# A transformer block with top-2 experts: normalisations moved to GpSimd, ranks by two products, and small changes of order

## The reference

```
x = x + attention(layernorm(x))      # 16 heads of 128, rope, causal softmax, output projection
x = x + ffn(layernorm(x))            # router over 8 experts, the best 2 of them, and a shared expert
layernorm(x) = (x - mean) / sqrt(var + 1e-5)
ffn(x):  scores = softmax(x @ gate_w.T); the top 2 scores, divided by their sum, weigh
         (silu(x @ w1[e]) * (x @ w3[e])) @ w2[e], experts 176 wide;
         plus (silu(x @ sw1) * (x @ sw3)) @ sw2, 352 wide
```

## Time and profile before

| what | value |
|---|---|
| median of 3 runs | 728.51 us (728.29 to 728.64) |
| time of the profiled execution | 729.91 us |
| its span, first to last instruction | 727.9 us |
| TensorE busy, products | 716.8 us, 98% |
| TensorE busy, weight loads | 690.7 us, 95% |
| VectorE / ScalarE / GpSimd busy | 617.2 (85%) / 526.8 (72%) / 506.2 us (70%) |
| mean granted clock of TensorE | 0.998 of full speed |

### The profile page before, as it was taken

One profiled execution on the slowest core, in us unless ns is written; L12 is line 12 of the kernel. 1 busy time (PEld: TensorE's weight loads), 2 busy tenths in 40 slices (PEclk: granted clock), 3 DMA queues, 4 the chain that ended last, 5 costly groups with the idle time before them and its releaser, 6 DMA issues.

```text
span 727.9 us, 16486 instructions
## 1 busy us (share of the span) xinstructions
PE 716.8 (98%) x5490; PEld 690.7 (95%) x5490; DVE 617.2 (85%) x1774; ACT 526.8 (72%) x1664; POOL 506.2 (70%) x531
## 2 busy tenths in 40 slices
PE   7999999999999999999999999999999999999997
PEld 6999999999999999999999999999999989999997
DVE  5888899989998999899989898989898976776657
ACT  5787777777777777777777777777777765666564
POOL 5898467787777777877777777777767623544545
PEclk9999999999999999999999999999999999999999
DMA  6555213221422143214321421131454373344383
GB/s 213 155 176 166 86 31 138 108 88 37 136 106 87 45 135 117 79 46 143 116 77 44 143 106 56 43 103 38 140 205 162 138 270 113 118 123 126 109 292 107
DMA packets 51211, 85.91 MB, mean 118 GB/s; under 512 B 8632, under 2 KB 43416, under 8 KB 49528
## 3 DMA queue, kind: packets, MB, share of 16 engines
q1 hardware_dynamic: 47080, 73.44, 30.3%
q0 software_dynamic: 4048, 11.42, 4.4%
HBM read 60.12 MB, written 44.59 MB: 144 GB/s over the span
## 4 chain that ended last, share of the span: by engine, by line
PE 80%; DVE 8%; POOL 6%; ACT 2%; issue 2%; DMA 1%; SPq 1%; POOLq 0%; DVEq 0%
PE bank L662 60%; PE bank L712 5%; PE bank L702 3%; PE bank L721 3%; POOL work L489 3%; DVE work L1104 2%; POOL rows_by_expert L1917 2%; DVE work L1097 1%; POOL qkt_lo L1788 1%; PE bank L954 1%; PE bank L935 1%; PE bank L704 1%; DVE xn L1261 1%; PE bank L849 1%; ACT work L1553 1%
## 5 line engine op out<-in xcount | busy, mean ns | idle before, releaser
L489 POOL TENSOR_TENSOR work<-work 128x512 f32<-128x512 f32 x127 | 164.9, 1298 | 52.7 <-DVE work L1104 51.9
L1788 POOL TENSOR_TENSOR qkt_lo<-work,qkt_hi 128x512 fp32r<-128x512 f32 x112 | 144.8, 1293 | 74.1 <-ACT qkt_hi L1546 74.1
L1104 DVE TENSOR_TENSOR work<-bank,sinn 64x512 f32<-64x512 f32 x256 | 176.2, 688 | 3.4
L662 PE MATMUL bank<-xnt_hi,w_lo 128*128 128x256 f32 x512 | 148.6, 290 | 0.8 <-DVE xnt_lo L1430 0.8
L662 PE MATMUL bank<-xnt_hi,w_hi 128*128 128x256 f32 x512 | 145.2, 284 | 0.0
L662 PE MATMUL bank<-xnt_lo,w_hi 128*128 128x256 f32 x512 | 145.2, 284 | 0.0
L1546 ACT CAST qkt_hi<-work 128x512 fp32r<-128x512 f32 x112 | 69.6, 622 | 87.3 <-POOL work L489 87.1
L1553 ACT ACTIVATE work<-work,bias 128x128 f32<-128x128 f32 (+1 forms) x256 | 112.7, 441 | 0.9 <-DVE bias L1113 0.9
L1097 DVE TENSOR_TENSOR work<-bank,cosn 128x512 f32<-128x512 f32 x128 | 88.0, 687 | 23.5 <-PE bank L662 23.2
L662 PEld LDWEIGHTS bank<-xnt_hi,w_lo 128*128 128x128 f32 x512 | 98.3, 192 | 1.7 <-DVE xnt_lo L1430 1.0
L662 PEld LDWEIGHTS bank<-xnt_hi,w_hi 128*128 128x128 f32 x512 | 98.6, 193 | 0.5
(11 more groups left out here) (205 smaller groups left out, 2125.3 us busy)
## 6 DMA issues: line engine op xcount, KB each, us to landing
rows_by_expert<-in_zero_t SPq DMA_DIRECT2D x17, 1028.0 KB
weights_split<-stage SPq DMA_DIRECT2D x40, 176.0 KB
w_lo<-weights_split SPq DMA_DIRECT2D x4, 1408.0 KB, 9.7
w_lo<-results_by_token SPq DMA_DIRECT2D x16, 256.0 KB, 5.3
w_lo<-rows_by_expert SPq DMA_DIRECT2D x24, 128.5 KB, 2.1
w_hi<-weights_split SPq DMA_DIRECT2D x2, 1536.0 KB, 6.4
stage<-in_L_ffn_w SPq DMA_DIRECT2D x32, 88.0 KB, 2.2
weights_split<-stage SPq DMA_DIRECT2D x20, 128.0 KB
```

The source lines that it names most:

```text
L489: eng.tensor_tensor(roped[:, a], rope_cos[:, a], rope_sin[:, a], ALU.add).then_inc(rope_add, 1)
L662: mm = pe.matmul(out, lhs[a], rhs[b], start=start and n == 0, stop=stop and n == 2, skip_group_check=more)
L1104: op = nc.vector.tensor_tensor(rope_sin[lo:lo + 64, a], p_qk[a][hi:hi + 64, :, :], sn, ALU.mult)
L1788: nc.gpsimd.tensor_tensor(qkt[a][1][:, :, :], roped[:, a], qkt[a][0][:, :, :], ALU.subtract).then_inc(qkt_lo, 1)
```

## The change

- The router's rows of sequence b-1 are normalised by GpSimd, the first half in head 3 and the second in head 4, each between rope sum and low part (in sequence 7 in heads 2 and 3). `rows_norm` on VectorE stays for the last sequence's rows alone.
- The next sequence's rows are normalised by GpSimd in head 10; VectorE keeps sequence 0 (`first_norm`). VectorE waits for the router's norm before it overwrites `mv` in head 5.
- `rsqrt` works in place; the tile `vare` goes.
- `ranks` takes two products instead of four. `member` gets eight more columns, the sum of both halves, by a second GpSimd add in `choose`; the second product reads first half and sum with a stride.
- 14 products on zeros follow the first values, before the scores of head 0.
- Order: in `closing` the low part and the cast of the shared expert's tile 1 come behind those of head 13's probabilities; behind it `low_s(0)`, `mult_s(2)`, `low_s(1)`, `low_x(0)` come before the statistics and aggregates; at the end the second scaled sum of the last tile comes behind `low_s` of that tile.

```diff
-RP = 7
+RP = 8
-WARM = 25
+WARM, AGAIN = 25, 14
-        member = sb("member", [P, ST * E], F32R)
+        member = sb("member", [P, 3 * E], F32R)
+        p_rest = [bank[a][:, E:3 * E] for a in (3, 4, 7)]
             def ranks(n, a):
-                pe.wait_ge(routed, (n - 1) * RP + 4)
+                pe.wait_ge(routed, (n - 1) * RP + 5)
-                first, second = member[:, 0:E], member[:, E:ST * E]
-                pe.matmul(p_rank[a], order[:, 0, :], member[:, :], start=True, stop=False)
-                pe.matmul(p_rank[a][:, E:ST * E], order[:, 1, :], first, start=False, stop=True)
-                pe.matmul(p_total[a], order[:, 1, :], first, start=True, stop=False)
-                pe.matmul(p_total[a], order[:, 1, :], second, start=False, stop=True).then_inc(rank_ps, 1)
+                pe.matmul(p_rank[a], order[:, 0, :], member[:, 0:ST * E], start=True, stop=False, skip_group_check=True)
+                pe.matmul(p_rest[a], order[:, 1, :], member[:, :].rearrange("p (t e) -> p t e", e=E)[:, 0:3:2, :],
+                          start=False, stop=True, skip_group_check=True).then_inc(rank_ps, 1)
+            for _ in range(AGAIN):
+                pe.matmul(bank[7][:, 0:S], pts[0][:, 0, :], pts[0][:, :, :], start=True, stop=True)
...
-                        if h == 2:
-                            rows_norm(b, b - 1)
                         if h == 5:
+                            wait(dve, xn2_done, b)
                             norm_mv(b + 1)
-                        if h == 9:
-                            norm_x(b + 1)
...
+            def row_norm(out, b, t):
+                return nc.gpsimd.tensor_scalar(out, resid[:, b * ST + t, :], mv[:, t, 0:1], rstd[:, t:t + 1],
+                                               ALU.subtract, ALU.mult)
...
+                    if b is not FIRST:
+                        if h + soon == 3 and b is not LAST:
+                            pool.wait_ge(rstd2_done, b)
+                            row_norm(xn2[:, 0, 0:D], b - 1, 0)
+                        if h + soon == 4:
+                            row_norm(xn2[:, 1, 0:D], b - 1, 1).then_inc(xn2_done, 1)
...
+                    if h == 10 and b is not LAST:
+                        pool.wait_ge(rstd_done, b + 2)
+                        row_norm(xn[:, 0, :], b + 1, 0)
+                        row_norm(xn[:, 1, :], b + 1, 1).then_inc(xn_done, 1)
...
+                            if b is LAST:
+                                pool.wait_ge(rstd2_done, b)
+                                row_norm(xn2[:, 0, 0:D], b - 1, 0)
...
+                pool.wait_ge(routed, (n - 1) * RP + 4)
+                nc.gpsimd.tensor_tensor(member[:, ST * E:], member[:, 0:E].bitcast(F32), member[:, E:ST * E].bitcast(F32),
+                                        ALU.add).then_inc(routed, 1)
...
             residual(LAST)
-            rows_stats(B, LAST)
-            rows_mv(B)
             low_s(0)
             mult_s(2)
             low_s(1)
+            low_x(0)
+            rows_stats(B, LAST)
+            rows_mv(B)
             mult_s(3)
-            low_x(0)
...
                 if t >= BY_POOL:
-                    finish(t)
+                    finish_first(t)
+                if BY_POOL <= t < NT - 1:
+                    finish_second(t)
             low_s(NT - 1)
+            finish_second(NT - 1)
```

More of the change, by code:

```diff
@@ L99, in build @@
         mv = sb("mv", [P, ST, 2])
-        vare = sb("vare", [P, ST])
         rstd = sb("rstd", [P, ST])
@@ L1082, in norm_mv, with first_norm @@
                 op.then_inc(mv_done, 1)
[L1084 to L1091, removed]
+            def first_norm():
+                dve.wait_ge(rstd_done, 1)
+                for t, done in enumerate((first_xn, xn_done)):
+                    nc.vector.tensor_scalar(xn[:, t, :], resid[:, t, :], mv[:, t, 0:1], rstd[:, t:t + 1],
+                                            ALU.subtract, ALU.mult).then_inc(done, 1)
             def rope_cosines(h):
@@ L1219, in closing @@
                 attended(12)
-                rows_low(1)
                 plan_tiles(0, 1)
                 probs_then_inverse(13)
+                rows_low(1)
                 biggest(15)
@@ L1294, in reduce_both @@
             def reduce_both(n):
-                dve.wait_ge(routed, (n - 1) * RP + 5)
+                dve.wait_ge(routed, (n - 1) * RP + 6)
                 nc.vector.tensor_reduce(red[:, :, :, :], prod[:, :, :, :].rearrange("p k c (t e) -> p (k c t) e", t=ST),
@@ L1410, in plan_tiles, with finish_first @@
                                                    ALU.add).then_inc(done, 1)
-            def finish(t):
+            def finish_first(t):
                 dve.wait_ge(came[t], 16)
@@ L1416, in finish, with finish_second @@
                                                ALU.mult, ALU.add).then_inc(fin_last, 1)
+            def finish_second(t):
                 dve.wait_ge(fin_last, 2 * (t - BY_POOL) + 1)
@@ L1425, in _ @@
             norm_mv(0)
-            norm_x(0)
+            first_norm()
             split_lo(0)
@@ L1623, in closing @@
                 attended(12)
+                probs_high(13)
                 rows_high(1)
-                probs_high(13)
                 scaled_by(14)
@@ L1781, in rsqrt @@
                 pool.wait_ge(ready_sem, count)
-                nc.gpsimd.tensor_scalar(vare[:, 0:n], mv[:, 0:n, 1], EPS, 1.0, ALU.add, ALU.mult).then_inc(step_sem, 1)
+                nc.gpsimd.tensor_scalar(rstd[:, 0:n], mv[:, 0:n, 1], EPS, 1.0, ALU.add, ALU.mult).then_inc(step_sem, 1)
                 pool.wait_ge(step_sem, count)
-                nc.gpsimd.tensor_tensor(rstd[:, 0:n], vare[:, 0:n], mhalf[:, 0:n], ALU.pow).then_inc(done_sem, 1)
+                nc.gpsimd.tensor_tensor(rstd[:, 0:n], rstd[:, 0:n], mhalf[:, 0:n], ALU.pow).then_inc(done_sem, 1)
+            def row_norm(out, b, t):
+                return nc.gpsimd.tensor_scalar(out, resid[:, b * ST + t, :], mv[:, t, 0:1], rstd[:, t:t + 1],
+                                               ALU.subtract, ALU.mult)
             def low(h):
@@ L1886, in choose @@
                 pool.wait_ge(pick_done, n)
-                nc.gpsimd.tensor_tensor(member[:, :], pick[:, 0, :], pick[:, 1, :], ALU.add).then_inc(routed, 1)
+                nc.gpsimd.tensor_tensor(member[:, 0:ST * E], pick[:, 0, :], pick[:, 1, :], ALU.add).then_inc(routed, 1)
+                pool.wait_ge(routed, (n - 1) * RP + 4)
+                nc.gpsimd.tensor_tensor(member[:, ST * E:], member[:, 0:E].bitcast(F32), member[:, E:ST * E].bitcast(F32),
+                                        ALU.add).then_inc(routed, 1)
             def weigh(n):
```

## The result

The changed kernel takes 731.78 us (median of 5 runs, 731.26 to 732.15), where the kernel before, run beside it, takes 728.51 us: ratio 1.0043, interval [1.003, 1.0055]. It is slower by 3.3 us; forecast was 718.8 us, range 716.9 to 722.3. Its profiled execution took 731.51 us, span 729.7.

What follows compares the result with a forecast made beforehand. TensorE's products were taken to bound the kernel nearly everywhere. 5.2 + 1.8 + 1.3 + 1.3 + 0.4 - 0.3 = 9.7 us off the profiled 729.91 gave 720.2, less 1.40 for the median 718.8; range 716.9 to 722.3.

Steps and rivals of the forecast that it cites:

- the price of the scaling: GpSimd's 128x256 scaling in heads 3, 4 and 10: taken as 0.75 us, between bounds of 0.19 and 0.83.
- the rival with its formula 4d - 3.64: GpSimd scaling far dearer: delay per sequence at price d, gain eaten from 1.26 us, 735.3 at 1.5; chance 0.03.
- signs of being wrong: Waits for GpSimd at heads 3 to 5 and 11 to 14, scaling over 1.2 us, or half rate after 14.5.
- the cover: Slack hiding GpSimd's delay: 0.73 us idle at head 3, 0.69 behind head 4's low part, 1.49 idle at head 10.
- a cover like the 0.69: Head 10: GpSimd 0.5 us later against TensorE was claimed to stay inside slack like that behind head 4's low part.
- Waits of TensorE that go, 5.2 us: TensorE's waits for VectorE's low probabilities: 0.62 in sequence 0, 3.5 at head 3, 1.1 at head 10, all going.
- Ranks, 1.8: Two of four rank products go, eight times 0.22 us, 1.8 us in all, counted in full.
- TensorE is the bound on both sides: Around the rank products TensorE sets the pace before and behind, so their 1.8 us counts in full.
- Idle products, 1.3: At the start 14 products hold the full clock from 14.4 to 18.0, gaining 1.3 us, ends 0 and 1.66.
- The rival: Clock at the start gives nothing, as timed runs kept it or 14 products don't hold it: 720.1 us; chance 0.15.
- Order, 1.3 + 0.4: Reordering gains 1.3 us at the last sequence's passage to the experts (0.35, 0.70, 0.25) and 0.4 at the end.
- Small waits, 0.3: Growing small waits at heads 0 to 2 through GpSimd's sends and sums cost 0.3 us, ends 0 and 1.2.

Runs made afterwards that it cites:

- e6: The kernel before with one dead 128x256 scaling added on GpSimd at head 10 of sequences 1 to 6: 728.18 us, ratio 0.9998.
- e7: The kernel before with two dead 128x256 scalings added on GpSimd at head 10 of sequences 1 to 6: 733.56 us, ratio 1.0068.
- e4: The kernel before with only the 14 products on zeros added: 728.59 us, ratio 1.0002.
- e11: The kernel before with only the ranks by two products and GpSimd's small second add: 727.70 us, ratio 0.9984.
- e12: The kernel before with only the other order, in and behind the last sequence and at the end: 727.11 us, ratio 0.9979.
- e1: The changed kernel with both normalisations back on VectorE at their old heads: 725.64 us, ratio 0.9959.
- e2: The changed kernel with only the next sequence's normalisation back on VectorE, at head 9: 726.91 us, ratio 0.9978.
- e3: The changed kernel with only the router's normalisation back on VectorE, at head 2: 730.72 us, ratio 1.0026.
- e5: The kernel before with ten dead GpSimd operations at its start, five forms at two widths, to time each form: 733.49 us in one execution.
- e8: The changed kernel with both norms on ScalarE, at heads 3 and 10, and a small per-row shift on VectorE: 727.51 us, ratio 0.9983.

## Why the prediction was wrong

The forecast was 13.0 us too low. The move of the norms accounts for 11.0 of it (a cost of 6.1 in place of a gain of 4.9), the idle products for 1.3, the ranks for 0.7.

**The step that failed first is the price of the scaling.** The bounds were 0.19 and 0.83, with 0.75 taken. It is 1.22 us, outside both. The lower row was nearly all start and the upper one an operation of another form; neither bounds a one-input operation with two steps. The bound should have reached past the two-input add, and the rival with its formula 4d - 3.64 should have had far more than 0.03. (A scaling "over 1.2 us" stood among the signs of being wrong, and it came.) At d = 1.22 that formula gives 1.24 us a sequence, 8.7 in all. That takes most of the gain and still ends as slightly faster (718.8 + 8.7 = 727.5), so the price alone does not explain 731.8.

**The second is the cover.** At head 3 I had looked for slack behind the low part of head 4 (0.69) and let head 3's delay run into it. But the scores that read head 3's low part come first. In before that low part ends at 180.69 + 1.29 = 181.98, and this is the load behind the wait for it (the first that reads the low part itself follows 0.22 us later):

```profile
182.44 0.30 PEld L702 LDWEIGHTS bank<-work 128*128 128x128 f32 x2
```

So there is 0.46 of cover, and 0.44 of it existed only because TensorE was itself waiting for `pt_lo` just ahead. Take that wait away and be 0.49 late (1.22 - 0.73): 0.49 + 0.44 - 0.46 = 0.47, the measured loss of head 4. The gain at head 3 was paid back one head later. At head 10 I named what is queued behind GpSimd ("the rope sum, ScalarE's cast, the low part") but allowed it a cover like that of the low part. The path that matters leaves it at the cast: behind the cast ScalarE's queue has the exponentials and `xnt_high`, and the chain above shows each begin as the one ahead of it ends (216.54, 217.16, 217.47, 217.87, 218.74). Then come VectorE's `xnt_lo` and TensorE's first projection of the next sequence, with 0.08 us of cover and not "a cover like the 0.69". Late by 2.44 - 1.49 = 0.95, TensorE earlier by the 0.38 it gained at head 10, less 0.08: 1.25, measured 1.26 over heads 11 and 12. e6 and e7 show it without the change.

**Waits of TensorE that go, 5.2 us: right as far as it went.** They went from 7.2 to 0.3. "All of it goes if nothing else is as late": something was, by up to 1.2 us.

**Ranks, 1.8:** the products went, 0.22 at each place; measured 1.1, since 0.19 came back at head 12 in six sequences (8 x 0.22 - 6 x 0.19 = 0.6 by the trace; the interval of the timing, 0.5 to 1.8, holds both). The second GpSimd add has 8 columns and not 16, and cost TensorE nothing that shows. "TensorE is the bound on both sides" was wrong on the side behind.

**Idle products, 1.3: nothing in the median.** The rival was right for its first reason: most timed runs kept their clock. The sum counted the same loss twice, once as 1.3 for the products and once in the 1.40 by which the median lies under the profiled execution. So this rival should have been the forecast. Whether the products help in the executions that do lose clock (20 of 109 without them, e4) was not tested by itself. The Trainium skill (TensorE: Matmul & The Clock Gate, Part 1: The HAM clock gate) warns that the switch falls differently from run to run, and the runs agree: of the profiled executions of before and of e6, e7, e11 and e12, all without the products, one shows 0.54 in this window and four show 1.00.

**Order, 1.3 + 0.4:** 1.7 measured alone, both waits and the gap at the end gone. The sum came out; how much each of its terms gave was not separated.

**Small waits, 0.3:** the group of L702 with "issue" (2.3 us, six times 0.4) was not foreseen. It goes when the next sequence's norm goes back (absent in e1 and e2, there in e3), so it too comes from the two scalings at head 10. In sequence 2 the load that waits starts at 218.64, 0.11 us after the end of GpSimd's low part (217.24 + 1.29 = 218.53), which is the likely releaser; TensorE waits longer still for `xnt_lo` just behind it, so this wait adds nothing of its own.

**The router's 1.1 us.** Heads 3 and 4 of sequences 1 to 6 sum to nearly the same with the router's norm on either engine. What moving it back saves lies elsewhere: 0.41 us at head 5 of sequences 3 and 6 together, and 0.15 at heads 3 and 4 of sequence 7 (10.57 against 10.42 us). From the first head to head 12 of sequence 7 the traces differ by 0.70. The rest of the 1.1 is within what the overlapping intervals allow.

**What was not tried:** the router's half on GpSimd together with the next norm on ScalarE, which the two best versions suggest. Nor was it tried to put the two waits of TensorE further back: both stand in front of loads that don't read the late tile, by 0.22 us for `qkt_lo` and by 0.24 for `xnt_lo`.

## What to carry to other kernels

A wait that goes can itself be the cover of the next one. When TensorE gets earlier by x and a helper later by y, look for x + y of slack at every reader downstream, and follow the queue of each engine that the late result passes through, not only the consumer of the result. Here covers of 0.46 and 0.08 us, small against the delays, let the move cost 6.1 us.

The price of an operation is taken from a row of the same form and width, or is measured by itself first. A row of a very small tile shows what an operation costs to start, and not what each element adds. Work is moved in the amount that the idle stretch holds: one scaling of 1.22 us into 1.49 us cost nothing, two cost 0.87 a sequence, and one half on each engine gave the fastest version.

## What the runs showed of the hardware

On GpSimd a `tensor_scalar` of 128x256 float32 takes 1.22 to 1.23 us with two per-row scalars (1.06 with two constants), double the two-input add of the same size (0.61) and three times its copy (0.39), all by e5. The Trainium skill (GPSIMD Engine Reference, 4.1 Engine selection) calls two-input operations there the slow ones against VectorE and one-input operations roughly line-rate; for this one-input operation the measurement decides against it: 1.22 us on GpSimd, 0.40 on VectorE undisturbed.

The same scaling on VectorE has no one price. The tile's instructions in before (count, shortest/median/longest ns) have the router's 16 between 0.40 and 1.15 us:

```profile
L1261 DVE TENSOR_SCALAR xn<-resid,mv,rstd x16: 402/410/1153, 106.9 to 608.5; 128x256 f32<-128x256 f32 x16
```

In the earlier trace rows two took 1.48 us from 178.95 on, while GpSimd's rope sum ran from 178.66 to 179.96:

```profile
178.66 1.30 POOL L489 TENSOR_TENSOR work<-work 128x512 f32<-128x512 f32 x1 [0.64 <-DVE work L1104]
```

The first of the two ended at 180.10, 0.15 us behind the rope sum, and the second took 0.40. So it is each time: in before 14 scalings began while a rope sum ran, and all 14 ended 0.15 us behind its end, whether that made them 0.54 or 1.15 us long. In e8 VectorE's shift of 128x2 took 1.02 us, from 177.27 to 178.29, while the rope sum ran from 176.98 to 178.27, and so did all 14 of its kind (1.01 to 1.02). Other instructions are not held up: the low part of the probabilities, of whose two inputs one lies in PSUM (`bank`), took 0.41 to 0.43 us all 63 times that it ran wholly beside a rope sum, as it does elsewhere, and the statistics, with one input, 0.41 to 0.42 all 13 times.

The Trainium skill (SBUF — State Buffer, 🔬 SBUF: two separate sides) has VectorE and GpSimd share a pair of ports as an exclusive lock: a VectorE instruction in a two-port mode, or with two inputs in SBUF, waits out a GpSimd instruction that began first. These rows agree with it, the unaffected ones too; no run here took GpSimd's work away to show it by itself. If it holds, 0.75 of the 1.48 us at head 3 was not the norm's own work (two undisturbed scalings take 0.73, at 608.21) but its place beside the rope sum. That is more than the 0.54 that TensorE waited there. Starting the norm at another time on VectorE is a rival to moving it, and it was not tried.
